# Batch statistics of images 0 to 7 between the second group's scans, and a pass that starts with image 0 instead of image 15

## The reference

```
xc = x * ca_gate                       # a gate per channel, from mean and max of the image
m = mean(xc, channels)                 # one number per pixel
y = _s6(m, ...)                        # h = a*h + b along the pixels of an image, 16 states
s = conv7x7([mean(xc), max(xc)])       # over the channels' mean and maximum
x2 = xc * sigmoid(y) + xc * sigmoid(s)
mean, var = mean(x2, (0, 1, 2)), var(x2, (0, 1, 2))      # needs every pixel of every image
out = relu((x2 - mean) * rsqrt(var + EPS) * bn_gamma + bn_beta)
return x1 + out
```

## Time and profile before

| | us |
|---|---|
| median of 3 runs | 3292.24 |
| the profiled execution, whole | 3285.82 |
| its span, first to last instruction | 3284.0 |
| block 1, to the last work before the meeting | about 1735.5 |
| block 2 before the first half sum | 1737.8 to 1820.9 |
| the statistics pass | 1820.9 to 2314.8 |
| block 3 with the last small work of block 2 | 2314.8 to 3284 |

### The profile page before, as it was taken

One profiled execution on the slowest core, in us unless ns is written; L12 is line 12 of the kernel. 1 busy time (PEld: TensorE's weight loads), 2 busy tenths in 40 slices (PEclk: granted clock), 3 DMA queues, 4 the chain that ended last, 5 costly groups with the idle time before them and its releaser, 6 DMA issues. The chain is left out here.

```text
span 3284.0 us, 50167 instructions
## 1 busy us (share of the span) xinstructions
PE 2531.5 (77%) x17105; PEld 1633.0 (50%) x17105; DVE 2971.8 (90%) x4057; ACT 2701.3 (82%) x3772; POOL 57.1 (2%) x111
## 2 busy tenths in 40 slices
PE   7899999999999999999987333333566766667776
PEld 5566666666666666666442000000455555555555
DVE  8789998999988999889986899999999999999997
ACT  6788888888888888888774688888799888888887
POOL 3000000000000000000001200000000000000000
PEclk9999999999999999999998555555688878787777
DMA  8899999999999999999866699999599999999998
GB/s 315 321 374 409 376 369 371 373 409 382 368 365 372 406 383 371 367 365 395 280 171 169 264 421 421 420 421 418 236 429 428 429 429 428 429 429 429 429 429 363
DMA packets 199097, 1228.49 MB, mean 374 GB/s; under 512 B 29792, under 2 KB 38936, under 8 KB 157644
## 3 DMA queue, kind: packets, MB, share of 16 engines
q1 hardware_dynamic: 195884, 1223.41, 92.4%
q0 software_dynamic: 2976, 2.00, 0.3%
HBM read 805.14 MB, written 420.17 MB: 373 GB/s over the span
## 5 line engine op out<-in xcount | busy, mean ns | idle before, releaser
L1449 PE MATMUL psum<-signs,taps 128*128 128x448 f16 x4032 | 856.5, 355 | 40.7 <-DVE signs L1078 31.8
L1568 PE MATMUL psum<-signs,picked 12*128 12x448 bf16 x896 | 314.5, 491 | 340.7 <-DMA signs<-gate_scratch 271.0
L1449 PEld LDWEIGHTS psum<-signs,taps 128*128 128x128 f16 x4032 | 385.2, 98 | 367.2 <-DVE signs L1078 51.3
L2001 DVE SCALAR_TENSOR_TENSOR xc<-xt,curs,psum 128x1792 f32<-128x1792 f32 x222 | 452.1, 2078 | 57.0 <-PE psum L1568 45.5
L841 ACT ACTIVATE xt<-psum 128x896 f32<-128x896 f32 x416 | 377.9, 910 | 143.6 <-PE psum L1347 129.7
L1781 DVE SCALAR_TENSOR_TENSOR xc<-xt,curs,psum 128x1792 f32<-128x1792 f32 x224 | 455.8, 2079 | 33.3 <-PE psum L1568 32.3
L1710 ACT ACTIVATE xc<-xc 128x1792 f32<-128x1792 f32 x224 | 380.1, 1697 | 95.2 <-DVE xc L1781 95.2
L1129 DVE CUSTOM_DVE_ANT_0 xt<-work,xt 128x896 f32<-128x896 int8 x416 | 436.0, 1086 | 13.7 <-ACT work L849 13.6
L1347 PE MATMUL psum<-ident,stage 128*128 128x128 f32 x3066 | 410.6, 276 | 22.0 <-DMA stage<-x_dram 12.3
L1972 ACT ACTIVATE xc<-xc,bn,curs 128x1792 f32<-128x1792 f32 x224 | 411.7, 1903 | 13.8 <-DVE xc L2001 4.7
L857 ACT ACTIVATE work<-xt,mean 128x1792 bf16<-128x1792 f32 x208 | 370.2, 1780 | 29.2 <-DVE x1max_p L1129 29.2
(11 more groups left out here) (221 smaller groups left out, 2953.2 us busy)
## 6 DMA issues: line engine op xcount, KB each, us to landing
xt<-x_scratch SPq DMA_DIRECT2D x210, 1792.0 KB, 25.3
stage<-x_dram SPq DMA_DIRECT2D x219, 896.0 KB, 10.0
xc<-x_scratch SPq DMA_DIRECT2D x210, 896.0 KB, 9.3
x_scratch<-xt SPq DMA_DIRECT2D x208, 896.0 KB, 9.3
out_dram<-stage SPq DMA_DIRECT2D x75, 1792.0 KB, 21.9
out_dram<-work SPq DMA_DIRECT2D x37, 1792.0 KB, 21.9
x_scratch<-last_unit SPq DMA_DIRECT2D x16, 896.0 KB, 10.2
signs<-ssm_scratch SPq DMA_DIRECT2D x14, 448.0 KB, 4.7
```

The source lines that it names most:

```text
L1449: return nc.tensor.matmul(turn[h % 2][:, b * 512:b * 512 + HB], taps[:, j, t, :], signs[:, j, r:r + RT // 2, dw:dw + W], start=t == 0, sto ...
L1568: last = nc.tensor.matmul(dst[:, b, :], picked[:, b * P:(b + 1) * P], gate_rows[:, s * BW:(s + 1) * BW], start=True, stop=True)
L2001: nc.vector.scalar_tensor_tensor(quarters(xc[m % 2][:, j, :]), slot_quarters(s, j), curs[:, h, j:j + 1], gate_quarters(gate_ps4), ALU.add, ...
```

## The change

Block 2 is put in another order:

- ACT issues the loads of image 0's first five strips into slots 0 to 4 as its first work. Slots 5 and 6 hold the five arrays of the delta steps (`px[1]` now lies in `last_slots`; it lay in `xc`) and are loaded once these are stored. Image 15 "keeps no place": it is loaded in its turn. The order is now 0, 1, ... 15, and all 112 strips are loaded instead of 105.
- SP loads the first group's y first of all. DVE does join, two delta steps, split, then the other six. The gate of image 0 is stored first (`store_first`, on SP), then loaded for seven slots, and only then SP stores the delta results and loads the rows for the scans.
- The half sums of strips 0 to 2 (`ALONE`) come before the scans, those of strips 3 to 9 go between them: scan, half sum, scan, half sum. The loads of strips 7 to 16 are issued by ACT (`reload`), after the squares of the strip whose slot they take.
- The scans have the first group's buffers, two for rows and three for factors. One PSUM buffer is left for `spread`, one for `read_out`, and one for the gate (`gate_middle`): the gate of the next strip waits until both half sums of the last are done.
- The second group's y is joined and split whole, around strip 12.
- Block 3 begins with image 15, which then lies in the slots.

```diff
-              [xcf[0][:, k * NQ:(k + 1) * NQ] for k in range(4)] + [xcf[1][:, 0:NQ]]]
+              [last_slots[:, k * NQ:(k + 1) * NQ] for k in range(5)]]
...
         def dx_ps(n):
-            return bank[2] if n < NCG else bank[n % 2]
+            return bank[2] if n < NCG else bank[0]
         def y_ps(n):
-            return bank[n % 2][:, 512:512 + YW] if n < NCG else bank[3][:, n % 2 * 512:n % 2 * 512 + YW]
+            return bank[n % 2][:, 512:512 + YW] if n < NCG else bank[3][:, 0:YW]
...
         def read_out(pe, n):
             pe.wait_ge(scanned, n + 1)
-            if n >= 2:
+            if n >= NCG:
+                pe.wait_ge(y_evac, n)
+            elif n >= 2:
                 pe.wait_ge(y_evac, n - 1)
...
+        ALONE = 3
+        SHARED = ALONE + NCG // 2
+            return gate_middle if isinstance(it, int) and n < SHARED else gate_ps3[n % 2]
...
             def _(sp):
+                load_y(sp, 0, 0)
                 load_m(sp, 1, px[1][0])
                 sp.wait_ge(pads_made, 3)
                 load_features(sp, 1)
-                load_y(sp, 0, 0)
+                store_first(sp)
+                sp.wait_ge(first_out, 16 * BR)
+                for s in range(NS):
+                    load_gate(sp, arrived3, 0, s)
                 for k, t, n in ((2, 4, 14), (1, 3, 15), (0, 2, 16)):
                     sp.wait_ge(delta_steps, n)
                     store_px(sp, 1, k, px[1][t])
...
             def _(act):
+                for s in range(NS - 2):
+                    act.dma_start(slots[s], x1_d[0, :, 2 * s:2 * s + 2, :, :]).then_inc(arrived3[s], 16)
...
+                for n in range(ALONE):
+                    if n == 2:
+                        act.wait_ge(ssm_out[1], 48)
+                        for s in range(NS - 2, NS):
+                            act.dma_start(slots[s], x1_d[0, :, 2 * s:2 * s + 2, :, :]).then_inc(arrived3[s], 16)
+                        make_decay(act, NCG)
+                        make_decay(act, NCG + 1)
+                    for j in range(NJ):
+                        square_half(0, n, j)
+                    if n == 0:
+                        copy_spatial(0)
+                    reload(n)
                 for n in range(NCG, NC):
                     if n + 2 < NC:
                         make_decay(act, n + 2)
                     if n > NCG:
                         evac_y(act, n - 1)
+                    m, j = ALONE + (n - NCG) // 2, n % 2
+                    square_half(0, m, j)
+                    if j == 1:
+                        reload(m)
...
             def _(dve):
+                join_y(0)
+                for k in range(2):
+                    delta_step(dve, 1, k)
+                split_gate(0)
+                for k in range(2, 8):
+                    delta_step(dve, 1, k)
...
+                for n in range(ALONE):
+                    for j in range(NJ):
+                        half_sum(0, n, j)
+                for n in range(NCG, NC):
+                    scan(dve, n)
+                    half_sum(0, ALONE + (n - NCG) // 2, n % 2)
+                for n in range(SHARED, NN):
+                    if n == NN - 2:
+                        join_y(1)
+                    for j in range(NJ):
+                        half_sum(0, n, j)
+                    if n == NN - 2:
+                        split_gate(1)
...
             def _(pe):
                 pe.wait_ge(conv_in, 64)
+                spatial_products(0, 0, 10)
+                spread_gate(0, 0, 0)
+                spatial_products(0, 10, 2 * KS)
+                for n in range(1, ALONE):
+                    spread_gate(0, n, n)
                 spread(pe, NCG)
+                spread_gate(0, ALONE, ALONE)
                 for n in range(NCG, NC):
                     if n + 1 < NC:
                         spread(pe, n + 1)
                     read_out(pe, n)
+                    k = 2 * (n - NCG)
+                    if k < 2 * KS:
+                        spatial_products(1, k, k + 2)
+                    m = ALONE + (n - NCG) // 2 + 1
+                    if n % 2 and m < SHARED:
+                        spread_gate(0, m, m)
...
```

More of the change, by code:

```diff
@@ L397, in binary_conv_then_gated_ssm_block, with store_first @@
         assert NROW * TC + 2 * YW + 3 * GW // 2 <= 4 * TP
[L400 to L413, removed]
+        first_out = sem("first_out")
+        def store_first(eng):
+            eng.wait_ge(split_made, 1)
             for a in range(BR):
-                eng.dma_start(gate_d[0, r0 // BR:r1 // BR, q, a * W:(a + 1) * W],
-                              split[1][r0 + a:r1:BR, q, (GI - 1) * W:GI * W]).then_inc(last_out[min(q, 1)], 16)
+                eng.dma_start(gate_d[0, :, :, a * W:(a + 1) * W],
+                              split[0][a:H:BR, :, 0:W]).then_inc(first_out, 16)
         def store_gates(eng, k, i0, i1):
-            eng.wait_ge(split_made, 2 * k + 1)
-            p0 = (k * GI + i0 + 1) % NB
+            eng.wait_ge(split_made, k + 1)
+            p0 = k * GI + i0
             for q in range(3):
@@ L1648, in _, with step @@
-                sp.wait_ge(gates_out, 48 * BR)
-                def step(it, more):
-                    for n in range(NN):
+                load_y(sp, 1, 0)
+                def step(it, n0, more):
+                    for n in range(n0, NN):
                         if n < NS or more:
                             sp.wait_ge(u_made3, it * (2 * NN) + 2 * (n + 1) + U3)
-                            load_slot(sp, arrived3, it * 2 + n // NS, it * 2 + n // NS + 1, n % NS)
-                step(0, True)
+                            load_slot(sp, arrived3, it * 2 + n // NS + 1, it * 2 + n // NS + 1, n % NS)
@@ L1683, in _, with square_half @@
+                nc.scalar.activation(s_out[0], s_out[0], ACT.Sigmoid).then_inc(s_sig, 1)
+                sigmoid_y(0)
+                act.sem_inc(squared3, Q3)
                 delta_exp(act, 1)
                 delta_log(act, 1)
[L1685 to L1688 removed]
+                def square_half(it, n, j):
+                    act.wait_ge(u_made3, it * (2 * NN) + 2 * n + j + 1 + U3)
+                    u = xc[n % 2][:, j, :]
+                    nc.scalar.activation(u, u, ACT.Square,
+                                         accum_out=g2_p[:, n, j, bass.ds(it, 1)]).then_inc(squared3, 1)
@@ new lines, in reload, with copy_spatial @@
+                def reload(n):
+                    if n < SHARED:
+                        act.dma_start(slots[n % NS], x1_d[n // NS + 1, :, 2 * (n % NS):2 * (n % NS) + 2, :, :]
+                                      ).then_inc(arrived3[n % NS], 16)
+                    if n == 2:
+                        act.wait_ge(gates_out, 48 * BR)
+                    if n >= 2:
+                        load_gate(act, arrived3, (n - 2) // NS + 1, (n - 2) % NS)
+                def copy_spatial(b):
+                    act.wait_ge(s_made, 3 + b)
+                    nc.scalar.activation(s_out[1][:, b * IB * W:(b + 1) * IB * W], s_ps[1][b], ACT.Identity
+                                         ).then_inc(s_raw, 1)
@@ L1831, in _, with spatial_products @@
             def _(pe):
-                def spatial_products(m0, m1):
-                    for m in range(m0, m1):
-                        b, k = m % 2, m // 2
+                def spatial_products(b, k0, k1):
+                    if b == 1 and k0 == 0:
+                        pe.wait_ge(s_raw, 2)
+                    for k in range(k0, k1):
                         last = convolve(1, b, k)
```

241 lines of the change are left out of this document (97 added, 144 removed).

## The result

| | before | after |
|---|---|---|
| median of the runs timed together, us | 3290.4 | 3311.91 |
| ratio, 95% interval | | 1.0081 [1.0067, 1.0095] |
| profiled execution, span, us | 3284.0 | 3309.4 |
| profiled execution, whole, us | 3285.8 | 3311.2 |

The change makes the kernel slower by 0.8%. 3293 was forecast, with 3273 to 3307 as the range; the time lies above it, nearest to rival (b).

The account below looks back on a forecast made before the run. The statistics pass was taken as bound by strip loads, 4.44 us each; 1764 + 19.4 + 16.2 + 66.5 + 30 gave T = 1896.1, 1.0 after break-even, so 3292.2 + 1.0, about 3293 us, range 3273 to 3307.

Parts of the forecast that it names:

- rival (b): Shared stretch slowed by short transfers or PE at 1.2 GHz: 11.5 us per strip, 3307; chance 0.24 with rival (c).
- The measure: Statistics pass: the last strip load lands at T + 413.8, so each us of T is a us of the result.
- T: Moment in block 2 when strip 13 has been used and the DMA engines never pause again; predicted 1896.1.
- break-even: Value of T, 1895.1, at which the last strip load lands as before, at 2308.9.
- Piece 1: Start of block 2: the first group's y lands at 1764, held by five strip loads; other end 1750.
- Rival (a): Start of block 2: strip loads do not hold y, which lands at 1750; 3279 us; chance 0.36.
- Pieces 2, 3 and 5: From y to first half sum, 19.4 us; strips 0 to 2, 16.2; last shared half sum to T, 30.
- D: Length of the shared stretch in block 2; predicted 66.5 us, with 57 below and 86 above.
- rival (c): Scans' inputs come late, first six half sums end long before the first scan, adding to D; chance 0.24 with rival (b).
- Piece 4: The shared stretch in block 2: 9.5 us per strip, so D = 66.5 us.
- shared stretch: Part of block 2 where seven strips' half sums run between 14 scans; predicted 66.5 us.

Follow-up runs that it names:

- e11: Changed kernel with only the first seven strip loads (image 0) cut to 64 bytes per partition, the ten reloads whole; 3277.91 us.
- e9: Changed kernel with each of ACT's 17 strip loads split into two transfers, packets of 3.5 KB in place of 14 KB; 3302.72 us, ratio 1.0048.
- e4: Changed kernel with all 17 of ACT's strip loads bringing only 64 bytes per partition; 3273.91 us.
- e12: Changed kernel with only the ten reloads cut to 64 bytes per partition, the first seven strip loads whole; 3287.79 us.
- e13: Changed kernel with products moved, strip loads staged one at a time, small packets, and the last four loads apart; 3297.35 us, ratio 1.0031.
- e5: Changed kernel with the second half's products (image 15's convolution) moved ahead of the shared stretch, the last four one to a strip; 3308.56 us, ratio 1.0073.
- e6: Changed kernel with the second half's products moved and the 17 strip loads cut to 64 bytes per partition; 3258.11 us.
- e1: Changed kernel with ACT's first five strip loads waiting until the first group's y has landed; 3304.97 us.
- e2: Changed kernel with the loads of strips 7 to 16 each issued three strips later, the last three together after the scans; 3321.21 us.
- e7: Changed kernel with products moved and strip loads staged between the small transfers, at most two under way; 3305.8 us, ratio 1.0062.

## Why the prediction was wrong

By its own steps:

- **The measure** (92 loads from T, break-even 1895.1, one us for one) is right to about 1 us: span - T is constant within 0.6 us over eleven kernels, and PE's last wait for a strip ended at 2334.62, where T + 413.8 gives 2335.4.
- **Piece 1** (y behind the strips' packets, 1764) held within 3.7 us. e11 shows the effect (1741.1 without the first loads) and e9 that it goes by the size of the packets. Rival (a) had 1750 and is refuted.
- **Pieces 2, 3 and 5** held within 3 us each. So the first scan's inputs were not late: D's loss begins at the third scan, and rival (c) did not happen.
- **Piece 4 failed.** "The row nearest to this is the high clock first, the low one later. I take 9.5 per strip: D = 66.5." It took 12.8 per strip, 16.5 in the first three and 10.0 in the last four. The clock was not high first: 0.54 from 1800 to 1845, where the first products are, so that row did not apply. Both ends named in the text were too low, 57 and 86; rival (b) named both causes, the short transfers behind the strips and PE at 1.2 GHz, at 11.5 per strip and 3307. The argument against (b), "only one strip is loaded per two chunks, so half of the factor loads go free", holds for the last four strips, where four of eight factors waited, and fails for the first three: five strips (7 to 9 and slots 5 and 6) are asked for between 1788 and 1802 us, just ahead of the first factors, and six factors in a row waited for their loads. The read-out then waited for the evacuation that stands behind them on ACT (6.04 us at 1818.49), the way that (b) describes. A chunk also has three more small transfers (two rows in, y out), and over the shared stretch their medians are 5.9, 6.6 and 6.4 us where e4 has 1.8, 1.8 and 3.5. With the reloads tiny D is 17 us shorter (e12), part of which is the clock.
- **The number** missed by less than T did. The forecast put 6.4 us on top of the profiled execution for its distance from the median; after the change that distance was 0.7. So the time is 18.9 over 3293 where T is 25.5 over 1896.1, and that is luck.
- **What should have been summed** is the DMA engines' own time. Before, from the start of block 2 to the break-even:

```profile
1737.00:1895.00 158.00, 82.65 (x296) 25.52 (x296) 126.48 (x118) 88.67 (x105) 27.04 (x46) 0.62 0.73 236
```

0.73 of 158 is 115.3 us of transfers, with 13 of the strips loaded by then. The change has to load 20 by T: 115.3 + 7 x 4.44 = 146.4 us. To break even, the engines would have to be busy 146.4 of 158 us, 93% of the time, through chains of small transfers that depend on one another. Windows from the block's start to T, of the kernel after, of e9 and of e13 (this one to 2.4 us past its T, since its last loads came late):

```profile
1737.00:1922.00 185.00, 91.40 (x286) 29.60 (x287) 107.35 (x100) 79.43 (x97) 14.38 (x23) 0.58 0.83 274
```

```profile
1737.00:1913.00 176.00, 89.74 (x284) 29.32 (x284) 107.08 (x97) 78.83 (x96) 13.64 (x22) 0.58 0.88 288
```

```profile
1737.00:1908.00 171.00, 93.88 (x288) 30.64 (x288) 109.49 (x100) 80.41 (x98) 16.31 (x26) 0.57 0.89 290
```

Busy 0.83 x 185 = 154, 155 and 152 us: the work of the transfers is the same within 2%, and the orders differ mainly in how much they leave idle, 31, 21 and 19 us. It is also 6 to 9 us more than the 146.4 worked out, so to break even takes 96 to 98% of the time; where these us come from is not shown. With none idle, 152 to 155 us would end at 1889 to 1892, 3 to 6 us or 0.1 to 0.2% better than before. That is worked out, not shown; what is shown is that eleven orders of the same transfers (after and the ten variants with whole loads) all stayed slower than before. The change puts work of DVE under other work, in a part where the DMA engines are busy 83 to 89% of the time and the small transfers take longer (the medians above), and it adds 7 loads (31 us) to them.

What stays open: how the 23 us of piece 4 divide between strips and clock. The differences depend on what else is in place (12.0 for the loads from after to e4, 22.3 from e5 to e6; 12.5 for the products from e4 to e6, 2.2 from after to e5), because each covers the other and because the granted clock differs between these kernels (0.50 in e4 from 1785 to 1830 us, 0.83 in e12 from 1812). No run held the clock fixed.

## What to carry to other kernels

When work is moved so that large loads run beside a chain of small transfers, sum the busy time of the DMA engines over the stretch first, and set it against the time there is: a plan that needs them busy 93% of the time, while every step waits for a round trip, did not fit here: 89% was the most that any order reached. Where one small transfer waits behind the large ones (y here), ask the same of every other one in the stretch; in e1, e2 and e7 the loads that were moved away from one met the next. And where two waits cover each other, an experiment that takes one away can show almost nothing (e5, 2.2 us): take both away, then each alone.

## What was not expected of the hardware

- PE busy 45.00 of 45 us at a granted clock of 0.50 (e4): being busy without a pause did not raise it, while in e12, with 5.41 of 10 us busy in one window, the clock in the next two was 0.83. The first is 1.2 GHz throughout, the second a mean of 1.2 and 2.4.
- Packets of 3.5 KB in place of 14 KB for the strip loads cost nothing that can be seen in the DMA engines' time (155 against 154 us until T), and brought y 14.7 us earlier and D down by 8.9 (e9).
- SP stands in line too: in the kernel after, its issue of two feature loads took 23.43 us while ACT's strips filled the DMA engines, 1.18 in e1, where they were not there yet:

```profile
1740.10 23.43 SPq L502 DMA_DIRECT2D stage<-feat_scratch  x2
```

```profile
1738.52 1.18 SPq L502 DMA_DIRECT2D stage<-feat_scratch  x2
```
